# A recurrent attention and expert block on one core: earlier copies and biases, six buffers for the norms, and the division behind the shared bank's reading

## The reference, cut to what matters

```python
x  = L0_attn_x                                  # 4 x 1024 x 128
xn = layernorm(x)
# attention: q = k = v = p, 16 heads of 8 columns
p = xn @ Wv.T + bv
attn = softmax(p_h @ p_h.T / sqrt(8))           # per batch and head, 1024 x 1024
s = concat_h(attn @ p_h) @ Wo.T + bo
# experts: 8 experts, 2 chosen per token
z = layernorm(xn) * ln_g + ln_b
probs = softmax(z @ rW + rb)
w = the two largest probs of a token, over their sum
hid = gelu(z @ W1[e] + b1[e])
mixed = sum_e w[e] * (hid @ W2[e] + b2[e])
g = silu(xn + mixed)
out = x + s * g
```

## Time and profile before

| | |
|---|---|
| median of 3 runs | 642.05 us (638.78 to 642.69) |
| the profiled execution | 640.8 us, of it 639.1 us from the first to the last instruction |
| busy in it: PE / ACT / DVE / POOL | 565.0 / 545.1 / 234.8 / 228.8 us |
| granted TensorE clock, mean | 0.928 of full speed |

### The profile page before, as it was taken

How to read it: one execution, slowest core, us unless ns; L and a number is a source line. 1 busy time by engine, 2 the same in 40 slices (tenths; PEclk the granted TensorE clock), 3 DMA queues, 4 the chain that set the end, 5 groups by cost and what they waited for, 6 DMA issues and landing times.

```text
span 639.1 us, 11460 instructions
## 1 busy us (share of the span) xinstructions
PE 565.0 (88%) x3982; PEld 227.1 (36%) x3982; DVE 234.8 (37%) x663; ACT 545.1 (85%) x597; POOL 228.8 (36%) x252
## 2 busy tenths in 40 slices
PE   3888389863699999979999999999997979999995
PEld 2642024210234344343444443434334334443321
DVE  5740786830233333212232222322232562222383
ACT  6879188854499999999999999999999969999994
POOL 2571047777777730047312221122103234342000
PEclk9978589878699999959999999999995989999998
DMA  6367941276454665434444435444333545351221
GB/s 162 123 199 218 412 157 51 76 185 180 102 119 99 144 149 114 101 90 119 102 129 112 138 79 143 102 119 117 91 120 103 137 136 162 110 158 55 77 73 40
DMA packets 101557, 81.54 MB, mean 128 GB/s; under 512 B 54083, under 2 KB 92502, under 8 KB 100694
## 3 DMA queue, kind: packets, MB, share of 16 engines
q1 hardware_dynamic: 94838, 71.26, 41.3%
q0 software_dynamic: 6656, 9.48, 4.5%
HBM read 57.03 MB, written 28.39 MB: 134 GB/s over the span
## 4 chain that ended last, share of the span: by engine, by line
PE 67%; DVE 8%; issue 7%; ACT 7%; DMA 6%; SPq 3%; POOL 2%; ACTq 0%; DVEq 0%
PE bank_v L1350 32%; PE pair L1298 15%; PE bank_f L1399 9%; PE bank_f L1390 8%; ACT exps L800 6%; DMA p_dram<-o_ring 2%; PE bank_f L1367 1%; DMA bo_bc<-in_L_attn_bo 1%; POOL o_ring L668 1%; DMA p_dram<-w_ring 1%; PE bank_f L1363 1%; DMA rows_in_sb<-o_dram 1%; DMA rows_in_sb<-in_L_attn_bv 1%; PE bank_f L1374 1%; DVE rows_in_sb L837 1%
## 5 line engine op out<-in xcount | busy, mean ns | idle before, releaser
L800 ACT ACTIVATE exps<-pair 128x1024 f32<-128x1024 f32 x512 | 489.7, 1051 | 75.2 <-PE pair L1298 57.2
L1350 PE MATMUL bank_v<-exps,v_tok 128*32 128x512 f32 x2048 | 285.5, 631 | 15.9 <-DVE o_turned L1103 15.0
L695 POOL DMA_INDIRECT o_dram<-o_ring,slot_place x80 | 77.1, 964 | 260.3 <-DVE o_ring L1154 259.7
L1298 PE MATMUL pair<-q_ring,k_ring 26*128 26x512 f32 x1024 | 153.1, 516 | 3.7 <-ACT exps L800 1.8
L1298 PEld LDWEIGHTS pair<-q_ring,k_ring 26*128 26x128 f32 x1024 | 60.6, 188 | 99.0 <-ACT exps L800 53.4
L680 POOL DMA_INDIRECT z_dram<-pre,dest_i x64 | 63.3, 989 | 55.0 <-DVE place_i L1058 35.8
L1399 PE MATMUL bank_f<-w_ring,pre 128*128 128x128 f32 x320 | 63.0, 325 | 13.6 <-ACT pre L776 5.5
L1399 PEld LDWEIGHTS bank_f<-w_ring,pre 128*128 128x128 f32 x320 | 46.6, 210 | 76.0 <-issue 42.4
L1390 PEld LDWEIGHTS bank_f<-zT,w_ring 128*128 128x128 f32 x320 | 42.5, 193 | 84.4 <-DVE pre L1145 43.4
L1390 PE MATMUL bank_f<-zT,w_ring 128*128 128x128 f32 x320 | 57.7, 304 | 16.2 <-issue 16.2
L1145 DVE TENSOR_TENSOR pre<-bank_f,w_ring 128x256 f32<-128x256 f32 x80 | 33.9, 423 | 104.0 <-PE bank_f L1390 102.2
(11 more groups left out here) (156 smaller groups left out, 269.5 us busy)
## 6 DMA issues: line engine op xcount, KB each, us to landing
w_ring<-w_dram SPq DMA_DIRECT2D x80, 192.0 KB
w_ring<-w_dram SPq DMA_DIRECT2D x80, 129.0 KB
q_ring<-p_dram SPq DMA_DIRECT2D x64, 104.0 KB
k_ring<-p_dram SPq DMA_DIRECT2D x64, 96.0 KB
z_dram<-s_tok SPq DMA_DIRECT2D x4, 1280.0 KB, 13.1
z_ring<-z_dram SPq DMA_DIRECT2D x80, 64.0 KB
rows_in_sb<-o_dram SPq DMA_DIRECT2D x16, 256.0 KB, 3.0
p_dram<-z_ring SPq DMA_DIRECT2D x12, 256.0 KB, 3.1
```

Of the source, the lines that this page charges most:

```text
L695: pool.indirect_dma_start(o_dram[:, :], bass.IndirectOffsetOnAxis(slot_place[:, h, 4 * k + i:4 * k + i + 1].bitcast(U32), 0), o_ring[:, q ...
L800: nc.scalar.activation(exps[:, g % ES, 2 * half:2 * half + 2, :], pair[(2 * g + half) % 3][:, :, :], ACT.Exp, scale=SCALE).then_inc(exp_do ...
L1298: ins = nc.tensor.matmul(pair[h % 3][:, j % 2, :], k_ring[32 * j:32 * j + KROWS, n % 2, kt * P:(kt + 1) * P], q_ring[32 * j:32 * j + KROWS ...
L1350: ins = nc.tensor.matmul(bank_v[32 * j:32 * j + 32, :], v_tok[:, (n // HG) * KT + kt, first:first + 32], exps[:, g % ES, j, :], start=(kt ...
```

## The change: what it does

- SP starts the loads of `rb` and `bo` in the prologue, right behind the tokens, and no longer behind the keys of unit 1 and W1.
- `keep_w2` and `clear_places` go to step 10 of SP's order (`KEEP_W2_AT`), from step 38, where they stood ahead of the first `load_z`.
- The routing of the first half stands two steps earlier, the "bias" uses start at step 13 and not 22, `scale_w1` stands at 17 to 22 and not 27 to 30, the norms start at 25 and not 27, the scatters, the places and all uses of the experts two steps earlier.
- Each of the six later norms has a buffer of its own, in `p_hi`, `p_lo` and `m_blk`. DVE waits only once, ahead of the first. The first `load_z`, which writes over `p_hi`, waits until all six are stored.
- `load_rows` stands at the head of a step in SP's order, no longer behind `load_unit` and the rest, and there are three steps and not two between it and `combine`.
- At a run's end DVE turns `bank_v`, reads the shared bank, and only then divides.

```diff
-RANK_AT = ((6, 6, 7, 7, 8, 8), (17, 18, 19, 20, 22, 23))
+RANK_AT = ((4, 4, 5, 5, 6, 6), (17, 18, 19, 20, 22, 23))
...
-BIAS_AT = 22
-COPY_HI_AT = 14
+BIAS_AT = 13
+COPY_HI_AT = 16
+KEEP_W2_AT = 10
...
-MOE_AT = 41
+MOE_AT = 39
...
-COMBINE_AT = [[g + 2 + i * 3 // 4 for i in range(HT)] for g in LOAD_AT]
+COMBINE_AT = [[g + 3 + i * 3 // 4 for i in range(HT)] for g in LOAD_AT]
...
+        def later_norms(g):
+
+            return (p_hi, p_lo, m_blk)[(g - EARLY) // 2][0:H, g % 2:g % 2 + 1, :]
...
             for c in range(3, len(X_CHUNKS)):
                 load_x(c)
+            sp.dma_start(rb_bc[:, :], rb.rearrange("(a d) -> a d", a=1).broadcast_to([P, E])).then_inc(bias_in, 16)
+            sp.dma_start(bo_bc[:, :], bo.rearrange("(a d) -> a d", a=1).broadcast_to([P, D])).then_inc(bias_in, 16)
...
             load_unit(1)
-            sp.dma_start(rb_bc[:, :], rb.rearrange("(a d) -> a d", a=1).broadcast_to([P, E])).then_inc(bias_in, 16)
             sp.dma_start(w1_stage, W1.rearrange("e h f -> h e f")).then_inc(w1_staged, 16)
-            sp.dma_start(bo_bc[:, :], bo.rearrange("(a d) -> a d", a=1).broadcast_to([P, D])).then_inc(bias_in, 16)
             zero_z(0)
...
             def store_norms(g):
 
                 sp.wait_ge(bank_f_read, written("norm", g))
-                sp.dma_start(p_dram[:, bass.ds(m_row, 1), g * BLK:(g + 1) * BLK], m_blk[:, g % 2:g % 2 + 1, :]).then_inc(m_kept[1 + g % 2], 16)
+                sp.dma_start(p_dram[:, bass.ds(m_row, 1), g * BLK:(g + 1) * BLK], later_norms(g)).then_inc(later_kept, 16)
...
                 h, k = divmod(q, QUADS)
+                if q == 0:
+                    sp.wait_ge(later_kept, (NB - EARLY) * 16)
                 if k == 0:
                     sp.wait_ge(scattered[h], HT * 2 * 16)
...
             for g in range(STEPS + 1):
                 n, k = divmod(g, US)
+                for h in range(HALVES):
+                    for i in range(0, HT, LOAD_TILES):
+                        if g == LOAD_AT[h] + i * 3 // 4:
+                            load_rows(h, i)
...
-                if g == SCATTER_AT[1] + 2:
+                if g == KEEP_W2_AT:
                     keep_w2()
                     clear_places()
...
                     g = arg[0]
-                    if g < EARLY + 2:
-                        dve.wait_ge(m_kept[0], 16 * EARLY)
-                    else:
-                        dve.wait_ge(m_kept[1 + g % 2], (g - EARLY) // 2 * 16)
-                    ins = nc.vector.tensor_scalar(m_blk[:, g % 2, :].bitcast(F32R), bank_f[0:H, :], -1.0, None, ALU.mult)
+                    if g == EARLY:
+                        dve.wait_ge(m_kept, 16 * EARLY)
+                        for i in range(2):
+                            dve.wait_ge(parts_stored[i], stored(NB - 2 + i))
+                    ins = nc.vector.tensor_scalar(later_norms(g).rearrange("h a n -> h (a n)").bitcast(F32R), bank_f[0:H, :], -1.0, None, ALU.mult)
...
                 for use in USES.get(g, []):
                     read_bank(*use)
+                if g >= VLAG and (g - VLAG) % KT == KT - 1:
+                    divide_out((g - VLAG) // KT)
                 beside(g)
```

More of the change, by code:

```diff
@@ L84 @@
 W2W = FC * D + D
-RANK_AT = ((6, 6, 7, 7, 8, 8), (17, 18, 19, 20, 22, 23))
-COUNT_AT = (11, 24)
-ASSIGN_AT = ((11, 12, 12, 13, 14), (25, 26, 27, 28, 30))
-SCALE_Z_AT = ((9, 10, 10, 11), (18, 20, 22, 23))
-EXP_AT = (14, 21)
-WEIGH_AT = ((15, 15, 16), (31, 32, 33))
-BIAS_AT = 22
-COPY_HI_AT = 14
+RANK_AT = ((4, 4, 5, 5, 6, 6), (17, 18, 19, 20, 22, 23))
+COUNT_AT = (9, 24)
+ASSIGN_AT = ((9, 10, 10, 11, 12), (25, 26, 27, 28, 30))
+SCALE_Z_AT = ((7, 8, 8, 9), (18, 20, 22, 23))
+EXP_AT = (12, 21)
+WEIGH_AT = ((13, 13, 14), (31, 32, 33))
+BIAS_AT = 13
+COPY_HI_AT = 16
+KEEP_W2_AT = 10
 BIAS_COLS = 4
-NORM_AT = 27
+NORM_AT = 25
 ZERO_AT = 8
-SCALE_W1_AT = (27, 28, 29, 30)
-SCATTER_AT = (15, 36)
-MOE_AT = 41
+SCALE_W1_AT = (17, 18, 20, 22)
+SCATTER_AT = (13, 34)
+MOE_AT = 39
 MOE_STEP = 1.19
 LOAD_LAG = 5
-PLACE_AT = (59, 82)
+PLACE_AT = (57, 80)
 BURST = 6
@@ L329, in build @@
         parts_stored = [sem(f"parts_stored{i}") for i in range(2)]
-        m_kept = [sem(f"m_kept{i}") for i in range(3)]
+        m_kept = sem("m_kept")
+        later_kept = sem("later_kept")
         m_row_ready = sem("m_row_ready")
@@ L465, in load_unit @@
                     sp.wait_ge(hi_copied, 32)
-                    for i in range(2):
-                        sp.wait_ge(m_kept[1 + i], (NB - EARLY) // 2 * 16)
+                    sp.wait_ge(later_kept, (NB - EARLY) * 16)
                 load_keys(n)
@@ L480, in _ @@
                         sp.wait_ge(n2_copied, e + 1)
-                        sp.dma_start(p_dram[:, M_ROW, e * BLK:(e + 1) * BLK], m_blk[:, e, :]).then_inc(m_kept[0], 16)
+                        sp.dma_start(p_dram[:, M_ROW, e * BLK:(e + 1) * BLK], m_blk[:, e, :]).then_inc(m_kept, 16)
                     for e in range(EARLY):
@@ L485, in _ @@
                     load_keys(0)
-                    sp.wait_ge(m_kept[0], 16 * EARLY)
+                    sp.wait_ge(m_kept, 16 * EARLY)
                     sp.wait_ge(m_zeroed, 32)
@@ L610, in _ @@
                         load_places(h)
-                    for i in range(0, HT, LOAD_TILES):
-                        if g == LOAD_AT[h] + i * 3 // 4:
-                            load_rows(h, i)
                 for q in range(HALVES * QUADS):
@@ L1104, in turn_out, with divide_out @@
                                     ).then_inc(o_turned_ready, 1)
+            def divide_out(m):
+                qh = m % QH
                 dve.wait_ge(o_turned_ready, m + 1)
```

## The result

The changed kernel takes 608.75 us, the median of 4 runs (608.17 to 609.3), against 641.65 (638.78 to 642.69) for the kernel before in the same session: a ratio of 0.949, 95% interval 0.946 to 0.953. Its profiled execution took 609.2 us with a span of 607.5; the span of before was 639.1, so there are 31.6 us to find.

What follows compares the result with a forecast made beforehand. A few long stalls were taken to bound the kernel: bo, a norm's store, the first quad's rows, a late row load. 640.8 less 31.0 at the first "up" and 5.3 at the fourth place gave 604.5, about 605; range 596 to 617.

Steps and rivals of the forecast that it cites:

- Early biases: Start of the second run: with bo loaded early, the 12.3 us wait for the first turn_out goes.
- Steps 10 to 38: Stretch up to the first "up": 56.4 us from the step rates, plus 4 us for DVE's lateness.
- DVE will not keep this pace: Steps 10 to 38: DVE's load makes PE wait for the bank, 4 us taken, bounds 0 and 8.
- a granted clock of 0.5 outside the two gelu stretches and the quad's wait: Sign named in advance that would show the prediction wrong, in PE's granted clock.
- The rival on the clock: Steps 10 to 90: PE's clock rests at the lower level, 0.87 us a step, about 675 us; chance 0.03.
- The norms: Later norms: six buffers end DVE's 4.57 us store wait and ACT's 6.00 us loss; the new wait costs nothing.
- `keep_w2` early: SP ahead of the first load_z: 12.0 us freed, but 7.5 us of the first quad's 15.2 us wait left.
- the price at the other end: W2 and b2 ahead of the p_dram copies: those end up to 12 us later, at no cost.
- Scatters: Half 0's 32 scatters start near 71, take 41 us, end near 112, hidden ahead of load_z.
- the third rival: Scatters wait for the copies, end at 137, first "up" at 143: 13 us more, 617 us; chance 0.07.
- The fourth place: At 510 to 520, rows for combine issued late behind SP's other loads: 5.3 us won, bounds 0 and 5.3.
- The division: At a run's end, dividing behind the bank's reading brings 0, at worst costs nothing.

Runs made afterwards that it cites:

- u_bias: The changed kernel with the loads of rb and bo put back behind the second unit's loads: 623.04 us, ratio 0.976 to the kernel before.
- b_bias: The kernel before with only the loads of rb and bo moved early, ahead of the zeros' stores: 629.72 us, ratio 0.982.
- p_wide: The changed kernel with the four bias products 64 columns wide instead of one, at the same place: 603.64 us, ratio 0.943 to the kernel before.
- u_norm: The changed kernel with the later norms back in two buffers: 613.8 us, ratio 0.961 to the kernel before.
- u_keep: The changed kernel with W2's copies and the clearing of the places back directly ahead of the first load of z: 621.55 us, ratio 0.971.
- p_z: The changed kernel with the first two quads' W1 loads at steps 30 and 31 and the first z load at step 33: 603.71 us, ratio 0.943.
- u_rows: The changed kernel with the experts' row loads at their old place in SP's step and combine one step earlier: 609.1 us, ratio 0.950.
- b_rows: The kernel before with only the row loads first in SP's step and combine one step later: 633.76 us, ratio 0.989.
- p_best: The changed kernel with 64-column bias products, the first quad's W1 loads at step 30 and first z load at step 33: 598.03 us, ratio 0.934.
- p_best_div: The kernel of p_best with the division back ahead of the shared bank's reading: 599.94 us, ratio 0.936 to the kernel before.

## Why the prediction was right, and where it was not

The forecast was 605 with 596 to 617; it came out at 608.75. (By its own sum, 604.5 and the 1.25 us to the median, it should have read 606.) The sum held since its three large terms are real and add up. Undone one by one, the early biases, the W2 copies' place and the norms' buffers put the first "up" 14.4, 14.4 and 4.0 us later. Less what each trace was late already ahead of its edit's place (0.7, 2.0 and 0.8 us: values at 59.43 for 58.73, 122.36 for 120.33, 103.30 for 102.48) that is 13.7 + 12.4 + 3.2 = 29.3, the 29.3 of the account; that it meets it to the tenth is chance, given the scatter.

- *Early biases.* "The first `turn_out` is then on time by 2.4 us": DVE waited 1.05 us for PE, and the values of the next run started at 60.73, forecast 61.4. Right; u_bias and b_bias show it alone.
- *Steps 10 to 38.* "DVE will not keep this pace", 4 us within 0 to 8: this step named the wrong cause. PE was free for the first "up" at 131.99 - 6.90 = 125.09, 64.4 us behind 60.73, where the rates alone gave 57.4 and the 4 us for DVE stood on top: 7 us are lost, not 4. p_wide gets 5.5 of them back (21.6 - 16.1) with DVE's work unchanged; there PE is free 58.6 us behind its own step 10 (120.23 and 61.62), so 1.2 us are left. The 5.5 were the clock; DVE's waits as such are in the small rest. That the sum came so close is luck in this term: 4 us set aside for DVE paid for most of what the clock took. My sign "a granted clock of 0.5 outside the two gelu stretches and the quad's wait" appeared. The rival on the clock had the place (steps 10 to 90) and the price (0.87 us a step) but the wrong trigger, PE's waits for ACT, and it went over seven steps, not eighty.
- *The norms.* Their wait is gone, and u_norm shows that the buffers are worth 3.2 us with the rest of the change in place, beside the 6.00 us of the earlier trace rows.
- *`keep_w2` early.* The 12.0 us freed ahead of z are right (12.0 in u_keep's queue). From the last norm's reading (113.43) to the first "up" it took 18.6 us, forecast 20.0 (0.5 to SP and 19.5); a wait of 6.90 was left, forecast 7.5. p_z confirms that SP's line made it. Mis-sized was the price at the other end: not 12 us of issue but 24.5, to 85.51. It cost nothing for the reason given: unit 2's loads had been issued by 91.2, and its step comes at 110.
- *Scatters.* First at 73.83, forecast "near 71", since the zeros landed late. The 32 of half 0 were issued in 42.3 us (73.83 to 116.13), forecast 41, most of them 1.26 us apart and none later than 2.2 us behind the one ahead, so the third rival did not come.
- *The fourth place.* Forecast 5.3, measured 3.5, and the reason given was only half of it. The rows no longer wait, but u_rows shows that the shift of the timetable by two steps does this without the edit, and b_rows that the edit does it without the shift (5.1 us there, as sized). Of the 1.8 us that are missing 0.8 lie behind the second gelu, where the clock came back one step later (values of 1.94, 1.94 and 1.47 us from 459.29, against 1.94, 1.85 and 1.07 from 491.07 before); the rest I could not place.
- *The division.* Forecast 0; the times cannot tell it from that. p_best and p_best_div show some 0.9 us at the norms, taken up behind them by the wait for z.

The miss of 4.7 us on the profiled execution (609.2 against 604.5) is thus 1.7 at the first "up", 1.1 between the halves, 1.8 at the end, and about 0.1 elsewhere. The first is the last norm, read 3.1 us late (113.43, forecast 110.3) by the clock at the biases, less the 1.4 us by which SP's line was shorter; the second is the clock behind the first gelu (one step more at the lower level: values of 1.94, 1.94 and 1.38 us from 251.25, against 1.94 and 1.19 from 284.18); the third is in part the same behind the second.

## What to carry to other kernels

When long waits go, look at what the engine does in the steps that close up behind them: products with a single column, in four consecutive steps, cost 5 us of clock here although TensorE hardly waited, and widening them cost 0.05 us a step. Where an engine waits for a load, follow the issuing queue back to the event that starts its line: moving other issues out of the way gained 12 us, and reordering the rest another 5, until the wait stood at the next quad. Before giving an edit credit for a wait that vanished, undo that edit alone: a shift of the timetable can change which loads of a fixed period stand in front.

## What the hardware showed unexpectedly

- TensorE's granted clock fell to the lower level (0.53 over 14 us) while the records have PE busy 13.73 of 14 us, with no wait above 0.91 us between 58 and the fall; with 64 columns instead of one in four products a wait of 0.87 us left it at 1.00. The Trainium skill ("TensorE: Matmul & The Clock Gate", section "Part 1: The HAM clock gate (the "warmup" mystery)") ties the clock to how busy the engine has been of late; the busy time in the records of 66 to 72, ahead of the fall, is 5.09 us in the changed kernel and 5.03 in p_wide, so it does not tell the two apart.
- SP's issues were not of fixed cost: the two copies of W2 took 15.65 us to issue at a DMA share of 0.96 (61 to 77), and 2.92 us and 3.02 us (u_keep) at 0.54 to 0.56. In the stretch at 1.00 (92 to 100) most of POOL's scatters still came 1.26 us apart.
